# A decoder layer with routed experts: a wait for each split of the weights, and another order of the half-size units

## What is computed

```python
# T = 4096 tokens, H = 512, M = 352, 32 experts, 6 for each token
g = ragged_dot(xs, w_gate, group_sizes)      # xs: the tokens sorted by expert
u = ragged_dot(xs, w_up, group_sizes)
d = ragged_dot(silu(g) * u, w_down, group_sizes)
expert_out = sum over the 6 of d * weight
shared = silu(x @ sw_gate) * (x @ sw_up) @ sw_down      # sw_*: 704 wide
out = x + expert_out + shared
```

## Time and profile before

| | us |
|---|---|
| median of three executions | 4454.72 |
| lowest and highest | 4450.11, 4465.22 |
| the profiled execution | 4499.0 |
| its span, first to last instruction | 4497.2 |
| TensorE (PE) busy | 4121.2 (92%) |
| DVE, ACT, GpSimd busy | 2867.4, 2257.8, 1485.9 |
| mean granted clock of TensorE | 0.968 |

### The profile page before, as it was taken

The page is one execution under the profiler, slowest core; times in us unless marked ns, Lnnn a source line. Parts: engine busy times, 40 slices in busy tenths (PEclk is TensorE's granted clock), DMA queues, the critical chain, the costliest instruction groups (busy, mean ns, idle before and its releaser), DMA issues.

```text
span 4497.2 us, 73509 instructions
## 1 busy us (share of the span) xinstructions
PE 4121.2 (92%) x24539; PEld 3069.3 (68%) x24634; DVE 2867.4 (64%) x6046; ACT 2257.8 (50%) x5261; POOL 1485.9 (33%) x1999
## 2 busy tenths in 40 slices
PE   7999999988988888888858999999999999999999
PEld 5777777753333333333327999999999989898998
DVE  3555555556777766776645777777777777775333
ACT  3555555545655555555533555555555555554111
POOL 0111111112233323332331555555555555553110
PEclk9999999989999989999978999999999999999999
DMA  4000000013333323333224888888888888886321
GB/s 171 20 20 20 20 20 18 15 48 94 104 97 105 95 92 97 97 98 97 92 76 134 238 244 246 246 244 242 245 244 246 243 246 249 240 248 191 108 79 63
DMA packets 289221, 617.45 MB, mean 137 GB/s; under 512 B 71584, under 2 KB 80160, under 8 KB 288848
## 3 DMA queue, kind: packets, MB, share of 16 engines
q1 hardware_dynamic: 221136, 453.83, 31.2%
q0 software_dynamic: 67136, 157.86, 15.1%
q10 hardware_dynamic: 576, 1.05, 0.1%
HBM read 461.81 MB, written 150.21 MB: 136 GB/s over the span
## 4 chain that ended last, share of the span: by engine, by line
PE 75%; DVE 10%; issue 5%; ACT 4%; POOL 3%; another core or an unknown queue 2%; DMA 1%; SPq 1%; ACTq 0%; DVEq 0%; POOLq 0%
PE ps L696 14%; PE ps L698 13%; PE ps L697 13%; PE ps L499 6%; DVE NM L1080 5%; PE ps L607 4%; PE ps L710 3%; PE ps L590 3%; PE ps L552 3%; PE ps L457 3%; PE ps L486 2%; ACT PX L843 2%; PE ps L736 2%; POOL MR L1423 2%
## 5 line engine op out<-in xcount | busy, mean ns | idle before, releaser
L696 PE MATMUL ps<-WG,XT 128*128 128x352 f32 x2416 | 809.1, 335 | 72.6 <-issue 54.2
L1080 DVE TENSOR_REDUCE NM<-ps 128x2 f32<-128x1024 f32 x512 | 622.7, 1219 | 336.4 <-PE ps L570 219.0
L698 PE MATMUL ps<-WG,XT 128*128 128x352 f32 x2416 | 783.3, 324 | 0.0
L697 PE MATMUL ps<-WG,XT 128*128 128x352 f32 x2416 | 780.5, 323 | 0.0
L843 ACT ACTIVATE PX<-ps 128x1024 f32<-128x1024 f32 x512 | 522.1, 1020 | 408.4 <-PE ps L590 298.1
L1526 POOL DMA_INDIRECT sum<-YO,TI x238 | 392.6, 1650 | 722.6 <-issue 675.5
L1271 DVE TENSOR_TENSOR HS<-ps,HS 128x352 f32<-128x352 f32 x302 | 158.5, 525 | 629.5 <-ACT HS L948 448.7
L696 PEld LDWEIGHTS ps<-WG,XT 128*128 128x128 f32 x2416 | 458.0, 190 | 100.8 <-issue 81.9
L801 ACT ACTIVATE PA<-ps,nb 128x128 f32<-128x128 f32 x1024 | 360.3, 378 | 281.1 <-DVE nb L1001 281.1
L948 ACT ACTIVATE HS<-ps 128x352 f32<-128x352 f32 x302 | 140.4, 465 | 686.4 <-PE ps L698 686.4
L1229 DVE TENSOR_TENSOR WG<-WL,WG 128x704 fp32r<-128x704 f32 x524 | 448.7, 883 | 18.9 <-ACT WG L922 18.2
(11 more groups left out here) (217 smaller groups left out, 8015.4 us busy)
## 6 DMA issues: line engine op xcount, KB each, us to landing
WL<-in_w_gate SPq DMA_DIRECT2D x127, 704.0 KB
WL<-in_w_up SPq DMA_DIRECT2D x127, 704.0 KB
DL<-in_w_down SPq DMA_DIRECT2D x127, 512.0 KB
kq_parts<-HL SPq DMA_DIRECT2D x64, 512.0 KB, 2.8
KS<-kq_parts SPq DMA_DIRECT2D x384, 64.0 KB, 2.6
QS<-kq_parts SPq DMA_DIRECT2D x384, 64.0 KB, 2.5
DL<-in_w_down SPq DMA_DIRECT2D x127, 192.0 KB
CB<-sum POOLq DMA_DIRECT2D x64, 256.0 KB, 3.1
```

The source lines that it names most:

```text
L696: pe.matmul(out_, lh(0), rh(0), start=first, stop=False)
L697: pe.matmul(out_, lh(0), rh(1), start=False, stop=False)
L698: return pe.matmul(out_, lh(1), rh(0), start=False, stop=last)
L1080: dve.tensor_reduce(NM[:, g % 2, qc, p:4:2], ps[:, 512 * bk:512 * bk + 1024].rearrange("p (i k) -> p i k", k=512), AX.X, ALU.max, negate=T ...
```

## The change

It does two things. `UNITS` puts single 111 + j behind pair 6j + 5, for j = 0 to 15, so that a single stands at every seventh place, and the last 15 units are pairs (96 to 110). And TensorE's one wait for all six splits becomes six: in `s2` one for each pair of chunks, ahead of chunks 0 and 2 of gate and of up, and in `s4` one ahead of chunk 0 (split 5) and one ahead of chunk 2 (split 6).

```diff
--- before.py
+++ after.py
@@ -10,7 +10,7 @@
 
 NBLK, NPAIR = 127, 111
 NONE = NBLK - NPAIR
-UNITS = [u for p in range(NPAIR) for u in [p] + list(range(NPAIR + p * NONE // NPAIR, NPAIR + (p + 1) * NONE // NPAIR))]
+UNITS = [u for p in range(NPAIR) for u in [p] + ([NPAIR + p // 6] if p % 6 == 5 and p < 6 * NONE else [])]
 ROOM = 4096
 NROW = 32 * ROOM
 LAMBDA_INIT = 0.8 - 0.6 * math.exp(-0.3 * 12)
@@ -714,13 +714,13 @@
                 kind, a, i, k = ITEMS[n]
                 q, xq = n % 2, C.turn[n] % 2
                 pe.wait_ge(S["v_xt"], C.turn[n] + 1)
-                if n == 0 or ITEMS[n - 1][3] < k:
-                    pe.wait_ge(S["v_sp"], 6 * k + 6)
                 if n >= 2:
                     pe.wait_ge(S["a_si"], n - 1)
                     pe.wait_ge(S["v_h"], n - 1)
                 for w in range(2):
                     for c in range(4):
+                        if c % 2 == 0 and (n == 0 or ITEMS[n - 1][3] < k):
+                            pe.wait_ge(S["v_sp"], 6 * k + 2 * w + c // 2 + 1)
                         m = three(bank(2 + q + 2 * w, 0, 352),
                                   lambda p: XT[:, xq, p, 128 * c:128 * c + 128],
                                   lambda p: WG[k % 2][:, p, w, c, :], c == 0, c == 3)
@@ -745,6 +745,8 @@
                     pe.wait_ge(S["v_y"], C.y[n - 1])
                 for c in range(3):
                     r = 128 if c < 2 else 96
+                    if c != 1 and (n == 0 or ITEMS[n - 1][3] < k):
+                        pe.wait_ge(S["v_sp"], 6 * k + 5 + c // 2)
                     m = three(bank(7), lambda p: HT[0:r, q, p, 128 * c:128 * c + 128],
                               lambda p: WD[k % 2][0:r, p, c, :],
                               c == 0 and not (kind == "s" and i == 1), c == 2 and not (kind == "s" and i == 0))
```

## The result

| | before | after |
|---|---|---|
| median of four executions | 4453.82 us | 4406.66 us |
| lowest and highest | 4450.11, 4465.22 | 4392.09, 4411.53 |
| the profiled execution | 4499.0 | 4411.53 |

The ratio is 0.9881, with a 95% interval of 0.9855 to 0.9907: the change takes off 53 us of 4454, between 41 and 65. That is faster, as forecast, and inside the range of 4354 to 4417, but 33 us short of the 4374 that stood as the likeliest.

What follows compares the result with a forecast made beforehand. TensorE was taken to bound the experts' stretch. 85.1 us of waits less 12.5 left over gives 72.6, plus 8.6 of clock is 81.2, off 4454.72 gives 4374 us; range 4354 to 4417, its own range 4362 to 4383.

Steps and rivals of the forecast that it cites:

- 85.1 us of waits: TensorE's 33 waits at the first gate matmul plus hidden idle at unit starts; 72.6 us of it forecast as gained.
- 8.6 of clock: Granted clock falling after four long waits at gate matmuls: 8.6 us, all taken as gained.
- The hidden 0.24 at each start behind a pair: New units after pairs: each start waits an unshown 0.24 us for the down splits; 96 starts, 23.0 us.
- That rival (0.04): Starts after pairs: the 0.24 is the change of buffers and stays, 23 us, giving 4397; chance 0.04.
- Gate matmuls need only the gate and up splits: Start of each unit: the first matmul needs only the first split; later splits at 0.82 us keep ahead of TensorE.
- HT after a single: First down matmul behind a single: HT comes late behind the two down splits, leaving 0.55 us 16 times, 8.8 us.
- the rival of late weights in this part (0.08): After singles and the unit behind: weights come late, DMA becomes the bound, eating 43 us, giving 4417; chance 0.08.
- what is left over: Waits remaining after the change: 8.8 us behind singles, 1.1 at the first unit, 2.6 at the last set; 12.5 in all.
- this rival (0.07): At the waits left, the granted clock falls each time, costing 28 us and giving 4402; chance 0.07.
- The added waits: In TensorE's stream at 161 places: 805 more waits, nearly all already met, taken to cost 0; upper bound 129 us.
- The two rivals of 0.08 and 0.16 us for a met wait: Added waits break matmul overlap: 0.08 each costs 64 us (4438), 0.16 costs 129 us (4503, slower); chance 0.04 each.
- three rivals: The nearer rivals: late weights 4417 (0.08), clock falls at waits left 4402 (0.07), 0.24 at pairs stays 4397 (0.04).

Runs made afterwards that it cites:

- e2: The new order of units with the one wait of before, in the kernel before: ratio 0.9992 to before, experts' time 2068.1 us.
- e1: The six waits with the old order of units: ratio 0.9881 to the kernel before, experts' time 2013.5 us.
- e6: The changed kernel with two waits (four gate and up splits; two down splits) in place of six: ratio 0.9895 to before, experts' time 2016.4 us.
- e3: The changed kernel with each gather of rows issued one item sooner, four ahead instead of three: ratio 0.9828 to before, experts' time 1989.6 us.
- e9: Changed kernel, gathers one item sooner, down splits behind HT during singles, last set's splitting paced over the item before: ratio 0.9784 to before, experts' time 1975.9 us.
- e10: The changed kernel run a second time, nothing altered: ratio 0.9876 to the kernel before, experts' time 2012.2 us.
- e8: The changed kernel with SP's weight load after each single held until GpSimd has worked out the late gather's rows: ratio 0.9913 to before, experts' time 2031.4 us.
- e7: The changed kernel with the six waits at all 302 items, 846 more met waits: ratio 0.9874 to before, experts' time 2010.1 us.
- e4: The changed kernel with the next unit's two down splits put behind HT during a single: ratio 0.9830 to before, experts' time 1989.7 us.
- e5: The changed kernel with gathers one item sooner and the next unit's down splits behind HT during a single: ratio 0.9808 to before, experts' time 1981.5 us.
- e11: The changed kernel with one weight load per single replaced by four small copies, so 16 units compute wrongly: experts' time 1996.9 us in one execution.

## Why the prediction was right, and where it fell short

**What bounds it, and the waits before.** Right. 85.1 us of waits and 8.6 of clock were predicted as what could be had, 93.7; the table has 92.2. The hidden 0.24 at each start behind a pair was a wait and was worth what was said: 18.8 us on 80 pairs before, 0.7 on 78 after. That rival (0.04) is out, by e2, which keeps it, and e1, which loses it.

**Gate matmuls need only the gate and up splits.** Right, down to the start 0.25 after L736 (0.24 in the rows above); e6 shows that it is nearly the whole of the change.

**HT after a single.** Right: 0.55 was forecast and 0.50 came. The two down splits and HT stand on DVE as they did in the earlier trace rows, to the hundredth:

```profile
2491.59 1.82 DVE L1238 TENSOR_TENSOR WD<-DL,WD 128x1024 fp32r<-128x1024 f32 x2 [1.09 <-ACT WD L931]
...
2494.76 0.61 DVE L1279 TENSOR_TENSOR HT<-ps,HT 128x256 fp32r<-128x256 f32 x2
...
2496.30 1.69 DVE L1231 TENSOR_TENSOR WG<-WL,WG 128x704 fp32r<-128x704 f32 x2 [0.15 <-ACT WG L924]
```

TensorE starts its down matmuls at 2495.43, 0.06 after HT and 0.50 after they could have started (2491.01 + 3.92).

**What else is late behind a single: the step that failed.** The list of what comes late next ended with HT. It looked at what TensorE reads in its next steps and not at what is issued late for two items on. On DVE the weights of the rows (L1254 in the old numbering) stand behind the same two down splits and the scaling of YO, on GpSimd the gather stands behind them and behind the scatter L1526. GpSimd's timeline after (L1528 is the scatter, L1505 to L1508 the row numbers, L1512 the gather):

```profile
2494.85 1.61 POOL L1528 DMA_INDIRECT sum<-YO,TI  x1 [4.19 <-issue]
2495.93 1.33 POOL L1505 TENSOR_SCALAR tg<-WR 128x1 f32<-128x1 f32 x1
2496.14 1.88 POOL L1506 TENSOR_TENSOR tg<-EI,CST 128x1 f32<-128x1 f32 x1
2498.13 0.34 POOL L1508 TENSOR_SCALAR TI<-tg,CST 128x1 int32<-128x1 f32 x1
2498.79 1.07 POOL L1512 DMA_INDIRECT XI<-x_normed,TI  x1 [0.32 <-DVE YO L1304]
```

and before, at a single, scatter and gather, with the transposes that use the gathered rows:

```profile
2650.37 1.61 POOL L1526 DMA_INDIRECT sum<-YO,TI  x1 [4.22 <-issue]
...
2651.67 0.76 POOL L1504 TENSOR_TENSOR tg<-EI,CST 128x1 f32<-128x1 f32 x1
...
2653.21 1.08 POOL L1510 DMA_INDIRECT XI<-x_normed,TI  x1 [0.33 <-POOL TI L1506]
```

```profile
2661.81 0.64 PE L710 MATMUL ps<-CST,XI 128*128 128x128 f32 x4
```

Before, the gather was issued at 2653.21 and used at 2661.81, 8.6 us later. After, it is issued at 2498.79, 5.4 us behind the end of the down splits where it was 4.3, and TensorE, now 2.0 us further on as counted from there, could have used it at 2504.32. It went on at 2505.60, 6.8 us after the issue. The lead of 8.6 had become 5.5. Of the 3.1 us that are gone, 2.0 are TensorE's stall, and 1.1 are GpSimd's own: from scatter to gather it needs 3.95 us (median of 16) where it needed 2.83, because the steps that work out the row numbers take longer. L1506 takes 1.88 us and ends at 2498.02, as DVE's two splits L1231 end (2497.99); before, the same step took 0.76, while DVE stood idle. That the splits, now earlier, hold up GpSimd is what these rows suggest; no run here shows it apart. The prediction named late rows nowhere; the nearest it had was the rival of late weights in this part (0.08), which did not come. Priced by the table, the pairs behind singles are 25.0 over, 8.8 forecast; with the first unit (2.6 against 1.1) and the pairs behind (2.0 against 0), that is 19.7 us of the 22.1 by which what is left over came out larger than forecast. e3, which gives the gather one item more of lead, takes back 19.8 us of experts' time.

**The end and the clock.** The last set waits 2.74 us as forecast (2.6), and the clock falls behind it:

```profile
4044.20:4049.70 5.50, 5.47 (x24) 5.50 (x25) 4.02 (x5) 2.45 (x4) 2.10 (x4) 0.69 0.52 101
```

24 matmuls in 5.5 us at 0.69, so 1.5 of the 8.6 us stay; e9, which has no wait there, gets them too. This step of the prediction did not hold together: it left a wait of 2.6 us at the last set and yet took the whole of the clock as gained. At the other waits of this execution, 0.1 to 1.8 us long, the clock does not fall. In the second profiled execution of the same kernel (e10) it falls once, behind one of the waits for XI:

```profile
3386.93 0.75 PE L710 MATMUL ps<-CST,XI 128*128 128x128 f32 x4 [2.18 <-DMA XI<-x_normed,TI]
```

```profile
3388.00:3391.50 3.50, 3.50 (x15) 3.50 (x14) 2.02 (x4) 2.11 (x5) 3.11 (x5) 0.52 0.96 337
```

That costs some 1.5 us: from 3388.04 on, 11 matmuls start 0.29 us apart and no longer 0.16. In e1 it falls behind a wait of 1.71, in e8 behind six of 1.7 to 2.2. So this rival (0.07), priced at 28 us for a fall at every wait that is left, is out at that price; its mechanism is not. For the short idles of the Trainium skill (TensorE: Matmul & The Clock Gate, A second HAM failure mode) the traces agree in part: over all kernels here eight of the 16 waits shown with 1.6 to 2.2 us were followed by a fall, and none of the 39 with 1.0 to 1.6, nor any at HT behind a single (0.3).

**The added waits.** Right at 0, as far as can be seen: e7 has 846 more and takes 0.7 us more than one execution of the changed kernel and 2.2 less than the other. The two rivals of 0.08 and 0.16 us for a met wait, the slower side among them, are out, and what the Trainium skill (TensorE: Matmul & The Clock Gate, Architectural detail) says of weight loads pulled ahead leads to no loss at a wait that is met.

**The weights.** They were not the limit yet. ACT waits for them 5 times, 5.7 us, unseen by TensorE. e4, e5 and e8 show how near it is: 20, 22 and 71 us of ACT's waits. In e5 one of them costs TensorE 1.7 us, in e8 they cost more than is saved at XI.

**The sum.** In experts' time 81.2 was forecast and 57.7 came (54.9 in e10). Of the 23.5 between, 22.1 are new waits and the clock at the end, and 1.5 is that there was less to be had. In the medians it is 47; by the ratio it is 53, between 41 and 65, which 57.7 lies within. The forecast's own range was 4362 to 4383, and 4406.66 lies outside it. It lies inside 4354 to 4417 because that range was made wide enough for three rivals, and none of the three is what came. That the range held is luck to this extent; what was right is the mechanism of the gain and its price at most places. The 87.5 between the two profiled executions holds 29.8 from the parts ahead; a forecast read off two spans would have been misled by it.

## What to carry to other kernels

Where one wait covers several results, split it where the first user needs only some: met waits cost nothing here, and two waits gave nearly all that six did. When a stall of the bounding engine goes, go through every queue that ran on during the stall, not only those that it reads next: whatever is issued there for later has lost that much lead. Compare each lead with how long that transfer takes in just that place, beside the large loads, and move the issue forward together with the stall.

## What was not expected of the hardware

A gather of 128 rows of 2 KB by GpSimd took 3.1 to 3.8 us from issue to last packet with no load of weights in flight, and 5.6 to 6.9 with one (medians by place in the order, from the DMA packets, in the kernel before, the changed one, e10 and e11). In the changed kernel the packets of the scatter issued at 2494.85 (128 of 2048 bytes) begin at 2500.2, when the packets of the gate and up weights issued at 2494.22 are through, and those of the gather issued at 2498.79 (64 of 4096 bytes) begin behind them, at 2503.1, and end at 2505.0.

After the waits of 2.49 us behind singles the granted clock fell from 2.4 to 1.2 GHz in two of fifteen cases before and in three of sixteen in e2, and after the wait of 2.5 shown at the last set in the changed kernel; in e8 it stayed up behind the same 2.5. Shorter waits were followed by a fall too: none of the 33 in the changed kernel (the longest 1.8), but one in e10 (2.18), one in e1 (1.71) and six in e8 (1.7 to 2.2). Over all kernels here that is eight of the 16 waits shown with 1.6 to 2.2 us, none of the 39 with 1.0 to 1.6, and five of the 31 with 2.25. So the length of the wait alone did not decide it.
